# A gated recurrence that begins with two steps of one block, and its weight loads in other places of the queue

## The reference

```python
def step(c, xt):
    ft = jax.nn.sigmoid(xt @ wf.T + c @ uf.T + bf)
    it = jax.nn.sigmoid(xt @ wi.T + c @ ui.T + bi)
    gt = jnp.tanh(xt @ wc.T + c @ uc.T + bc)
    c = ft * c + it * gt
    return (c, None)
c_final, _ = lax.scan(step, c0, x)
h = jnp.tanh(jnp.einsum('tbi,oi->tbo', x, wo) + c_final @ uo.T + bo)
```

## Time and profile before

| | us |
|---|---|
| median of 3 runs | 2647.38 |
| lowest, highest | 2645.84, 2648.0 |
| span of the profiled execution | 2645.3 |

### The profile page before, as it was taken

One profiled execution on the slowest core, in us unless ns is written; L12 is line 12 of the kernel. 1 busy time (PEld: TensorE's weight loads), 2 busy tenths in 40 slices (PEclk: granted clock), 3 DMA queues, 4 the chain that ended last, 5 costly groups with the idle time before them and its releaser, 6 DMA issues.

```text
span 2645.3 us, 57571 instructions
## 1 busy us (share of the span) xinstructions
PE 2527.1 (96%) x22659; PEld 2205.2 (83%) x22659; DVE 1839.7 (70%) x3415; ACT 1621.4 (61%) x3003; POOL 1124.1 (42%) x1433
## 2 busy tenths in 40 slices
PE   5499999997899999999999999999999999999998
PEld 4278888886788888888888888888888888888887
DVE  7855556547887677776777887777677774467667
ACT  8657667566655555555556665555555554378777
POOL 7768687725332123222224342222222320067667
PEclk9799999998999999999999999999999999999999
DMA  8779797889774455445665755544556432489998
GB/s 348 294 227 310 266 316 268 272 292 335 195 196 116 125 141 164 127 116 125 146 161 153 193 162 142 162 130 116 124 142 159 131 85 49 156 337 347 369 360 347
DMA packets 507551, 542.52 MB, mean 205 GB/s; under 512 B 273936, under 2 KB 412944, under 8 KB 488720
## 3 DMA queue, kind: packets, MB, share of 16 engines
q1 hardware_dynamic: 507280, 538.85, 65.5%
HBM read 292.88 MB, written 180.88 MB: 179 GB/s over the span
## 4 chain that ended last, share of the span: by engine, by line
PE 84%; DVE 4%; POOL 4%; ACT 4%; DMA 2%; issue 2%; SPq 1%; DVEq 0%; POOLq 0%; ACTq 0%
PE bank L2150 31%; PE bank L2160 29%; PE bank L2206 8%; PE bank L2039 4%; PE bank L1989 3%; PE bank L2025 3%; PE bank L2047 2%; PE bank L2001 2%; PE bank L2181 2%; DVE big L1831 1%; PE bank L2009 1%; POOL big L890 1%; ACT big L1345 1%; POOL big L994 1%; DVE big L1888 1%
## 5 line engine op out<-in xcount | busy, mean ns | idle before, releaser
L2150 PE MATMUL bank<-big 128*128 128x256 f16 x8064 | 1081.2, 274 | 18.6 <-ACT big L1391 8.0
L2160 PE MATMUL bank<-big 128*128 128x256 f16 x7056 | 962.4, 273 | 0.0
L2150 PEld LDWEIGHTS bank<-big 128*128 128x128 f16 x8064 | 791.6, 98 | 116.4 <-ACT big L1391 9.7
L2160 PEld LDWEIGHTS bank<-big 128*128 128x128 f16 x7056 | 690.4, 98 | 79.9
L1035 POOL TENSOR_SCALAR big<-big 128x1 f32<-128x1 f32 x253 | 107.7, 426 | 1092.3 <-DVE big L1678 810.1
L1888 DVE TENSOR_TENSOR big<-bank,big 128x512 f32<-128x512 f32 x256 | 174.8, 683 | 196.9 <-PE bank L2160 193.8
L2206 PE MATMUL bank<-big 128*128 128x256 f16 x2688 | 295.3, 273 | 4.4 <-ACT bank L1325 4.0
L1301 ACT ACTIVATE big<-big 128x512 f32<-128x512 f32 x384 | 289.6, 803 | 14.0 <-DVE big L1888 11.9
L2206 PEld LDWEIGHTS bank<-big 128*128 128x128 f16 x2688 | 262.4, 98 | 36.9 <-ACT bank L1325 4.9
L1874 DVE TENSOR_TENSOR big<-bank,big 128x512 f32<-128x512 f32 x256 | 176.1, 688 | 142.8 <-PE bank L2160 119.1
L1233 ACT ACTIVATE big<-big 128x512 f32<-128x512 f32 x256 | 205.9, 808 | 104.4 <-POOL big L1037 101.1
(11 more groups left out here) (234 smaller groups left out, 3712.1 us busy)
## 6 DMA issues: line engine op xcount, KB each, us to landing
xtd<-big SPq DMA_DIRECT2D x60, 1024.0 KB, 6.9
big<-xr SPq DMA_DIRECT2D x16, 2048.0 KB, 9.1
big<-xg SPq DMA_DIRECT2D x64, 512.0 KB, 7.6
big<-kpad SPq DMA_DIRECT2D x32, 1024.0 KB, 12.1
yd<-big SPq DMA_DIRECT2D x16, 2048.0 KB, 16.8
big<-x SPq DMA_DIRECT2D x128, 256.0 KB, 3.3
x1d<-big SPq DMA_DIRECT2D x128, 256.0 KB, 3.2
big<-x1d SPq DMA_DIRECT2D x64, 512.0 KB, 8.8
```

The source lines that it names most:

```text
L2150: ins = e.matmul(o, WX[2 * g + lw][:, q, kt, 128 * a:128 * a + 128], slot[u % 2][:, part, lx, k0 + kt, :], start=(first and kt == 0 and (l ...
L2160: ins = e.matmul(o, WC[2 * g + lw][:, q, kt, 128 * a:128 * a + 128], cc[unit(u)[1] % 2][:, qc, lx, kt, :], start=False, stop=end, skip_gro ...
```

## The change

`ORDER` now begins with (0,0), (1,0), (0,1), (2,0), (1,1), (3,0), (2,1) and so on to (7,0), (6,1); from place 15, (0,2), the order is as before. So unit 1 is the second step of block 0 and needs the state of unit 0. For this, at n = `BEHIND` = 6 (the first group of unit 1):

- TensorE does k3 and k7 of group 5 ahead of everything of group 6;
- ACT does the gates of group 4, two steps of preparation, the gates of group 5, two more, and then all of `state_high(0, ...)`; DVE likewise the gates of group 5, the new state and all of `state_sums(0, ...)`;
- the state product waits for only as many low parts as it reads.

WX 4, WX 5 and WC 0 are loaded right after `load_y(0)`, the other WC parts in one piece behind the x rows of unit 1. The tables for units 1 to 5 are new, and POOL makes the row sums for units 1, 3 and 4 (before: 1 and 2) beside 16 to 19.

```diff
-ORDER = [(b, j) for b in range(7) for j in (0, 1)] + [(7, 0), (0, 2), (7, 1), (0, 3)] + [(b, j) for b in range(1, 8) for j in (2, 3)]
+ORDER = [(0, 0), (1, 0), (0, 1)] + [p for b in range(2, 8) for p in ((b, 0), (b - 1, 1))] + [(0, 2), (7, 1), (0, 3)] + [(b, j) for b in range(1, 8) for j in (2, 3)]
+BEHIND = 6
...
-        "act": ((1, 0), (1, 1), (1, 2), (2, 0), (2, 1), (2, 1), (2, 2), (2, 2), (3, 1), (3, 2), (4, 0), (5, 1), (6, 0), (6, 0), (6, 0), (6, 0))},
+        "act": ((1, 0), (1, 1), (1, 2), (2, 0), (2, 1), (2, 1), (2, 2), (2, 2), (3, 1), (3, 2), (4, 0), (5, 1), (6, 0), (6, 0), (6, 1), (6, 1))},
...
-POOL_SUMS = (1, 2, 16, 17, 18, 19)
+POOL_SUMS = (1, 3, 4, 16, 17, 18, 19)
...
+                if i == NG:
+                    w.wait_ge(s["cv"], G * (NG - 1))
+                    load_y(0)
+                    w.wait_ge(s["wx"], 16 * 4)
+                    load_WX(4)
+                    load_WX(5)
+                    load_WC(0)
...
-            w.wait_ge(s["wx"], 16 * 4)
-            load_WX(4)
-            load_WX(5)
             w.wait_ge(s["w_lo"], low_base(8))
             w.wait_ge(s["wd"], stored(7))
             w.wait_ge(s["fb"], 12)
-            load_WC(0)
             load_WC(1)
+            load_WC(3)
+            load_WC(4)
+            load_WC(5)
...
-                    if v == last + 2:
+                    if v == (16, 18)[j]:
...
+                if n == BEHIND:
+
                     gates(n - 2)
+                    for step, v in ACT_AT[n, 0]:
+                        prepare(step, v)
+                    gates(n - 1)
+                    for step, v in ACT_AT[n, 1]:
+                        prepare(step, v)
+                    for part in range(3):
+                        state_high(0, part)
...
-                    if u >= 2:
+                    if unit(u)[0] or unit(u)[1] >= 2:
...
+                if n == BEHIND:
+
+                    for step, v in DVE_AT[n, 0]:
+                        prepare(step, v)
+                    gates(n - 1)
+                    new_state(n - 1)
+                    for step, v in DVE_AT[n, 1]:
+                        prepare(step, v)
+                    for part in range(3):
+                        state_sums(0, part)
...
-                    w.wait_ge(s["clo"], state_parts(last_unit(u)))
+                    w.wait_ge(s["clo"], state_parts(last_unit(u)) - 6 + (1, 1, 2, 3, 4, 5, 6)[qc])
...
+                if n == BEHIND:
+
+                    w.wait_ge(s["k5"], n)
+                    step(n - 1, 3, bank_b(n - 1)[:, 256:512], False, "p3")
+                    w.wait_ge(s["k6"], n)
+                    step(n - 1, 7, bank_a(n - 1)[:, 0:256], False, "p7")
```

More of the change, by code:

```diff
@@ L600, in load_WC, with load_y @@
                 e.dma_start(WC[n].rearrange("p q k f -> p q (k f)"), wg[2 * g + 1][:, l]).then_inc(s["wc"], 16)
+            def load_y(v):
+                b, j = unit(v)
+                src = yd[:, :, b, 4 * j:4 * j + 4, :].rearrange("g t k h -> t g k h")
+                if v == 0:
+                    w.wait_ge(s["y0"], 16 * 7)
+                    w.wait_ge(s["y1"], 16 * 7)
+                    e.dma_start(yt[:, 0:NG - 2], src[:, 0:NG - 2]).then_inc(s["yl"], 16)
+                    return
+                w.wait_ge(s["y0"], 16 * 8)
+                w.wait_ge(s["y1"], 16 * 8)
+                if v == 1:
+                    w.wait_ge(s["yc"], 2)
+                elif v == 2:
+                    w.wait_ge(s["x1"], 4)
+                    w.wait_ge(s["yl"], 32)
+                else:
+                    w.wait_ge(s["ss"], 8 * v)
+                    w.wait_ge(s["xh"], 8 * v - 2)
+                    w.wait_ge(s["xlo"], 8 * v - 2)
+                e.dma_start(rows_y(v), src).then_inc(s["yl"], 16)
             e.dma_start(sm, small).then_inc(s["sm"], 16)
@@ L1371, in act_program @@
                 late = n % 3 in (0,)
-                if not late and 2 <= n <= GROUPS + 1:
+                if n == BEHIND:
                     gates(n - 2)
-                if 1 <= u <= NU and gi == 2:
+                    for step, v in ACT_AT[n, 0]:
[5 more added lines that the diff above has]
+                        state_high(0, part)
+                if not late and 2 <= n <= GROUPS + 1 and n != BEHIND + 1:
+                    gates(n - 2)
+                if 2 <= u <= NU and gi == 2:
                     state_high(u - 1, 0)
-                if n < GROUPS + 6:
+                if n < GROUPS + 6 and n != BEHIND:
                     for step, v in ACT_AT[n, 0]:
@@ L1393, in act_program @@
                     head_first(m)
-                if late and 2 <= n <= GROUPS + 1:
+                if late and 2 <= n <= GROUPS + 1 and n != BEHIND:
                     gates(n - 2)
-                if 1 <= u <= NU and gi == 2:
+                if 2 <= u <= NU and gi == 2:
                     state_high(u - 1, 1)
-                if n < GROUPS + 6:
+                if n < GROUPS + 6 and n != BEHIND:
                     for step, v in ACT_AT[n, 1]:
@@ L2228, in pe_program @@
                     step(n, 1, A[:, 0:256], False, "pa")
-                if n:
+                if n and n != BEHIND:
                     w.wait_ge(s["k5"], n)
```

55 lines of the change are left out of this document (16 added, 39 removed).

## The result

| | before | after |
|---|---|---|
| median, us | 2647.07 (4 runs) | 2660.89 (4 runs) |
| lowest, highest | 2645.84, 2648.0 | 2659.59, 2662.15 |
| span of the profiled execution | 2645.3 | 2657.9 |

The ratio is 1.0054, 95% interval 1.0043 to 1.0066: slower by 13.8 us. The forecast was 2644.8 in a range of 2637 to 2653, with 0.16 for slower. It was wrong, by 16 us.

What follows compares the result with a forecast made beforehand. TensorE, busy 96% of the span, was the bound, losing time mainly while the first two units run. Unit 2's end: 651.3 + 83.9 + 8.6 + 1.8 + 1.2 = 746.8 against 749.4, so 2644.8 us, range 2637 to 2653.

Steps and rivals of the forecast that it cites:

- Step 1: WX 4, WX 5, WC 0 right behind load_y(0): load_y(1) and ACT's two evictions shift by 6.7 us, bounds 0 and 7.5.
- T: End of p6 of group 5 (product k6) on TensorE: 644.6 in the kernel before, forecast 651.3.
- Step 2: WC 1, 3, 4, 5, 2 in one stretch before unit 1's rows are ready: costed at nothing.
- Step 3: Unit 1 needs unit 0's state at once: 8.6 us stall (bounds 7.1 and 12), then 1.8 us of half clock.
- Step 4: Unit 1's 55 us of TensorE work covers preparation of unit 2; the earlier 11.3 us of losses there go.
- Step 5: Unit 2, (0,1), with 27.5 us of TensorE work and the end of preparation 3: loses 1.2 us, bounds 0.5 and 11.3.
- rival B: Unit 2, groups 12 to 17, is starved as unit 1 was: loss 11.3 instead of 1.2, 2654.9 us; chance 0.14.
- Step 6: From unit 3 on, order and tables are a unit's shift of the old; TensorE stands nowhere: nothing.

Runs made afterwards that it cites:

- staging: Changed kernel, weight loads nearly as before: none behind load_y(0), five behind unit 1's x rows, WC 3, 4, 5 behind its fourth x1d store; 2655.16 us.
- the earlier tables: Changed kernel with other tables: preparation 2 cut in groups (6,3) to (9,3), preparation 3 ending at (14,2) instead of (15,2); 2654.23 us.
- Moving the early statistics: Changed kernel with other tables for preparations 2 and 3 and staged loads, plus preparations 4 and 17 begun later; 2647.39 us against 2646.96 without that.
- the cut of VectorE's work: Sums and splits of unit 1's state cut to 4 of 256 columns: 2660.82 us in the changed kernel, 2652.05 with other tables for preparations 2 and 3.
- the gap loads: Changed kernel with other tables for preparations 2 and 3, its three early loads sent in the idle stretch ahead of load_y(0); 2653.07 us.

## Why the prediction was wrong

**Step 1, the loads ahead: right in chain, a little too large.** load_y(1) came 5.2 us later instead of 6.7, and T, counted from load_y(0), 4.4. Put into the kernel before, the loads cost 5.6 us; staging, which also moves three WC loads, takes 5.7 off the changed one. That the wait for `wg` was covered anyway, so that the price had no return, is what the step had said.

**Step 2, the WC loads in one stretch, at nothing: as far as can be seen right, with three loads ahead.** The changed kernel, with WC 3, 4 and 5 in that stretch, has T at 63.8 us, and the kernel before with the three loads ahead and WC 3, 4 and 5 among the turns has it at 65.1. With the three put back (eight in a row) it no longer holds: the x1d stores were late and unit 0 lost more than load_y(1) gained.

**Step 3, the state stall: right.** From T (647.5 in the trace) to 661.60 TensorE lost 10.2 us; stall and half clock were forecast at 10.4. The turned rows released it at T + 7.8 (T + 8.3 forecast), and the first state product began at T + 10.8, behind VectorE's split (T + 10.5 forecast). The stretch from 655.28 to 661.60 has a granted clock of 0.54, near the lower of its two levels, as the earlier trace rows has it (0.53) after its wait.

**Step 4, unit 1 covers preparation 2: right.** 48.40 us without a gap, VectorE busy for 30.57 of them.

**Step 5 failed: "It has the shape of places 15 and 17, with the same tables less 90 groups", 1.2 us.** It lost about 15.5. The matmuls have that shape, and the tables of preparations 4 and 5 are those of 19 and 20 less 90 groups. But preparation 3 is not 18 less 90: that would begin at (9, 2), and it begins at (10, 3), because preparation 2 ends at (10, 2), two groups later than 17 less 90. At place 15 the request for unit 17's y rows goes out at (91, 3) and their first statistic is at (93, 3); here both fall between (10, 2) and (10, 3). VectorE's stop of 4.7 us came at the end of unit 1, where TensorE had cover, and was paid in unit 2, where VectorE was busy 40.50 of 47.10 us and couldn't catch up. The tables that took the stop away took off 6.7 us (8.5 between T and the end of unit 2). This is rival B's place, and only in part its mechanism: the larger part went with tables that leave the same work in unit 2, so it was no matter of the amount, and what the traces show is VectorE stopped by a transfer that was asked for too late (no run moves that request alone). The prediction counted VectorE's work in that stretch and never asked when load_y(3) would go out, though SP's queue was read for load_y(1).

What is left is, at least in part, rival B's own mechanism, VectorE's load in a unit with half the matmuls. In the changed kernel at 744 to 748 its order shows it: the next y statistic, two low parts of the state and two products, and ACT's eviction waits behind them.

```profile
744.46 0.69 DVE L1691 BATCH_NORM_STATS2 big<-big 128x6 f32<-128x512 f32 x1 [0.69 <-DMA big<-yd]
...
745.28 1.27 DVE L1737 TENSOR_TENSOR big<-big 128x512 f16<-128x512 f32 x2
746.47 1.28 DVE L1796 TENSOR_TENSOR big<-big 128x512 f32<-128x512 f32 x2
```

```profile
747.25 0.60 ACT L1405 ACTIVATE big<-bank 128x512 f32<-128x512 f32 x1 [1.87 <-DVE big L1796]
```

Some 7 us are left there with the earlier tables (15.5 less 8.5). The state's parts were shown to make 2.2 of them by the medians, 3.3 by the traces. Moving the early statistics shortened a wait by 0.8 without any gain in time, and the rest was not taken apart.

**Step 6 failed: "order and tables are a unit's shift of the old ones ... Nothing".** The shift ends at place 15, and there the unit before is another one. It cost 4.85 us (29.78 for 24.93): the waits (3.38 for 0.52) and the lower clock behind the second (54 matmuls in 7.73 us, where 6.07 is the full rate; the granted clock is 0.58 from 1442.15 to 1446). Without the state's parts that are made there, it is 25.61.

**The sum by steps**, from load_y(0): T +4.4; from T to place 15, where both have the same matmuls and all the losses lie before the end of unit 2, +4.75 (25.7 lost for 20.9); place 15 +4.85. That is 14.0, against 13.8 in the medians. The forecast had +6.7, -9.3 and 0. The gain that the new order was to bring, a state stall of 10.4 in place of 20 us of losses, did come; unit 2, place 15 and the loads ahead gave back more than that.

## What to carry to other kernels

When an order of work is shifted, compare what stands on both sides of each seam, not only the shape of the piece itself: the cost was at the two places where a short unit got another neighbour. For each engine that will be tight in a stretch, ask also when the transfers that it needs are requested, and by whom that request is held. And of two costs that stand partly one behind the other, the one that is taken away alone can look like nothing: the cut of VectorE's work was worth 0 in the medians while the transfer was late, and 2.2 us once it wasn't.

## What the runs showed of the hardware

**More bytes through a full queue.** From 586 to 610 the engines moved 388 GB/s with the loads between (share 1.03) and 368 without. The three loads, 2.75 MB, put load_y(1) off by 5.2 us in the change and by 5.9 in the kernel before, so the delay is less than their bytes would take at 408 GB/s, the rate that I had used: it answers to 470 to 530 GB/s (an estimate, bytes by delay, and no rate that a row shows). Either these large rows moved faster than that stretch's mean, or part of the time before load_y(1) hangs on something else than bytes; no run tells the two apart. The Trainium skill's page "DMA: Bandwidth & Descriptors", Specifications, gives about 358 GB/s as one core's share of HBM. The rows of this core, 368 to 408 GB/s, lie above it.

**What a wait costs beside itself.** The 54 matmuls of the last group of unit 2 took 6.07 us behind a wait of 2.22 with the earlier tables, and 7.74 behind one of 2.22 in the kernel with the gap loads too; behind 3.60, in the changed kernel, they took 8.68. The granted clock is 1.00 from 744.16 to 750 in the first, 0.71 from 743.55 to 746.50 and 0.81 up to 751 in the second, and 0.50 from 747.90 to 752 in the third. The row of the second:

```profile
743.55 7.74 PE L2176 MATMUL bank<-big 128*128 128x256 f16 x54 [2.22 <-ACT big L1407]
```

So a wait of this length can cost up to three quarters again by the clock, and it can't be told from its length alone whether it does. I had expected it only after the long stall. The Trainium skill's page "TensorE: Matmul & The Clock Gate", What's actually happening, says that throttled is the default and activity releases it. The third stretch agrees with it: a granted clock of 0.50 behind the wait, and 0.85 from 752 to 756.4, once TensorE had worked again.
